# Additions first in VectorE's turn, in the three later edge stages of a four-layer graph network

## The chip, the cores and the metric

The kernel runs on one core of a Trainium2 chip. The metric is the device time in microseconds (us); of the kernel before there are three timed runs, and one more execution was profiled. A core has five engines that run side by side and wait for each other by semaphores: TensorE (PE in the profile, with PEld for its weight loads), VectorE (DVE), ScalarE (ACT), GpSimd (POOL) and SyncE (SP).

## The reference

Four layers, each a graph layer and a dense mixer side by side and then a feed-forward part. The edge sums of layers 1 to 3 are what the change touches (the mixer and feed-forward parts are left out here):

```
xn = _layernorm(x)
# layer 1, relation graph: a weighted mean by (relation, target)
msg = xn[src] * edge_weight[:, None]
h = segment_sum(msg, edge_type * N + dst) / count ;  out = einsum('rnc,rco->no', h, weight) + xn @ root + bias
# layer 2, isomorphism graph
agg = segment_sum(edge_weight[:, None] * xn[src], dst)
# layer 3, graph attention
h = xn @ W ;  e = exp(-leaky_relu((h @ a1)[src] + (h @ a2)[dst], 0.2))
h_prime = segment_sum(e[:, None] * h[dst], src) / segment_sum(e, src)[:, None]
```

There are 3125 nodes of 256 values and 50000 edges.

## The kernel before, in words

The nodes are cut into 25 tiles of 125 (`P`). The edges are sorted by the tile of the node that they are summed into, and padded, so that a run of 512 edges (`by_dst`, grain 512) or of 256 (`by_src`, grain 256) belongs to one tile. A group is 512 edges, 4 units of 128 (`GT` = 4). `edge_stage` (line 1346) goes over the groups three times in the program: as `g1e` (mode "relation", 124 groups), as `g2e` (mode "weight", 124 groups) and as `g3e` (mode "gat", 110 groups). With grain 512 a group has one sum (`sums` = 1), with grain 256 it has two (`sums` = 2).

For a group, these steps are made:

- POOL gathers the rows of the 4 units from DRAM by indirect DMA (line 1418), into one of six buffers (`GOTS` = 6). A buffer is free again when the sums of the group six before it are complete (`summed`).
- VectorE makes one-hot rows of the edges' target nodes (`place`, line 1562). TensorE turns them (`pt`, line 1460), ScalarE brings them to SBUF (`placet`, line 1444), and TensorE fetches with them each edge's value of its tile (`pq`, line 1488). From `pq` VectorE works out one coefficient for each edge (lines 1536 to 1540 in mode "gat", 1544 to 1553 in mode "relation", called the coefficients below), and ScalarE multiplies the one-hots by it (`placew`, line 1437; in mode "gat" after an exponential, line 1431). In mode "weight" none of this is needed: VectorE makes `placew` itself in 4 instructions (line 1527).
- TensorE multiplies: `pa` (PSUM, `adds` = 2 banks in turn) becomes the sum over the units of `placew`, turned, times the gathered rows (line 1474). This is the sum.
- VectorE adds the sum from PSUM to the node tile in SBUF (line 1575, the addition). The tile's number was loaded to a register before (line 1566).

The order is written out by hand, as a software pipeline over turns n. In turn n TensorE does `pt` of group n+3, `pa` of n, `pq` of n+2, and a step of a mixer. ScalarE does `placew` of n+1, `placet` of n+3, and a step of the mixer. VectorE does the coefficients of n+1 (or `placew` of n+2), `place` of n+4, the additions of n-1, and a step of the mixer. The mixer (`side`: `SoftmaxMixer`, `HeadNormMixer`, `SquaredMixer`) is a coroutine that is advanced one step by each engine in each turn; its tiles are named `m_...`.

The waits around the addition are these. VectorE's addition of sum x waits for `summed` x+1, and TensorE's `pa` of sum x waits for `added` x-1, since with two banks it writes over sum x-2. So with one sum to a group, `pa` of group n waits for the addition of group n-2; with two sums to a group (`g3e`), the first half of `pa` of group n waits for the first addition of group n-1. The coefficients of n+1 wait for `pq` of n+1, which stands behind `pa` of n-1 in TensorE's program, and `pq` of n+2 waits for the coefficients of n+1, as it has one PSUM buffer. `placew` of n+2 in mode "weight" waits for the sum of n-1.

Of the kernel before, what the change touches and what calls it, by code (L numbers as in the profile page):

```python
# [18 lines left out]
ALU = mybir.AluOpType  # L19
ACT = mybir.ActivationFunctionType  # L20
AX = mybir.AxisListType
ds = bass.ds
# [3 lines left out]
NT = N // P  # L26
# [592 lines left out]
def advance(program):  # L619

    if program is not None:
        next(program, None)


def run_out(program):

    if program is not None:
        for _ in program:
            pass
# [716 lines left out]
def edge_stage(nc, R, name, mode, b, acc, width, table, idx=R_IDX, spread=None, side=None, clear=True):  # L1346
# [10 lines left out]
    groups = b.units // GT  # L1357
    each = b.grain // 128
    sums = GT // each
    wide = table.shape[1]  # L1360
    PART = -(-groups // PARTS)
    turns, adds, ahead = 1, 2, 5
    with ExitStack() as ctx:
        def sem(n):
            return nc.alloc_semaphore(f"{name}_{n}")
# [22 lines left out]
        pa = [ctx.enter_context(nc.psum_tensor(f"{name}_pa{k}", [P, 512], F32)) for k in range(adds)]  # L1388
# [3 lines left out]
        split, placed, weighed, turned, evacuated, spreaded, logit, summed, added = (sem(n) for n in names)  # L1392
        block = ctx.enter_context(nc.Block())

        def fetched(g):

            return got_in[g % GOTS], 16 * GT * (g // GOTS + 1)

        @block.sync
        def _(sp):  # L1400
            view = b.rec[0:b.units * 128, :].rearrange("(p u) r -> p u r", p=128)
            for c in range(PARTS):
                at = slice(c * PART * GT, min(b.units, (c + 1) * PART * GT))
                sp.dma_start(rc[:, at, :], view[:, at, :]).then_inc(rec_in[c], 16)
            if side is not None:
                side.sync(sp)
            for c in range(PARTS):
                sp.wait_ge(rec_in[c], 16)
# [85 lines left out]
        @block.vector  # L1494
        def _(dve):
            tile_regs = [dve.alloc_register(f"{name}_dve_tile{k}") for k in range(sums)]
            own = side.vector(dve) if side is not None else None
            if clear:
                dve.memset(acc, 0.0)
            dve.tensor_copy(identb[:, :], R.identf[:, :])  # L1500
            if spreads:
                whole = spread.rearrange("p (t e) -> p t e", e=sw)
                dve.tensor_copy(rest[:, :, :], whole)
                dve.drain()
                for piece in range(3):
                    dve.tensor_copy(pieces[:, :, piece, :], rest[:, :, :])
                    dve.drain()
                    if piece < 2:
                        dve.tensor_tensor(rest[:, :, :], rest[:, :, :], pieces[:, :, piece, :], ALU.subtract)
                        dve.drain()  # L1510
                dve.sem_inc(split, 1)
            dve.drain()

            def ready(g):

                if g % PART == 0:
                    dve.wait_ge(rec_in[g // PART], 16)

            for n in range(1 - ahead, groups + 1):
                g = n + 2  # L1520
                if mode == "weight" and 0 <= g < groups:
                    ready(g)
                    if g >= 3:
                        dve.wait_ge(summed, (g - 2) * sums)
                    for j in range(GT):
                        u = g * GT + j
                        dve.tensor_scalar(placew[:, g % 3, j, :], R.iota[:, 0:P], rcf[:, u, b.loc:b.loc + 1],
                                          rcf[:, u, R_W:R_W + 1], ALU.is_equal, ALU.mult)
                    dve.drain().then_inc(weighed, 1)
                g = n + 1  # L1530
                at = slice(g * GT, (g + 1) * GT)
                if spreads and 0 <= g < groups:
                    dve.wait_ge(spreaded, g + 1)
                    if mode == "gat":
                        dve.wait_ge(*fetched(g))
                        dve.tensor_reduce(coef2[:, g % 4, :], pq[g % turns][:, 0:GT, 0:3], AX.X, ALU.add)
                        dve.drain()
                        dve.tensor_tensor(coef[:, g % 4, :], coef2[:, g % 4, :], got[:, g % GOTS, :, wide - 1], ALU.add)
                        dve.drain()
                        dve.scalar_tensor_tensor(out=coef[:, g % 4, :], in0=coef[:, g % 4, :], scalar=0.2,  # L1540
                                                 in1=coef[:, g % 4, :], op0=ALU.mult, op1=ALU.max)
                    else:
                        rels = [128, GT, 8]
                        dve.tensor_tensor(rel[:, g % 2, :, :], R.iota[:, 0:8].rearrange("p (a e) -> p a e", a=1).broadcast_to(rels),
                                          rcf[:, at, R_REL:R_REL + 1].broadcast_to(rels), ALU.is_equal)
                        dve.drain()
                        dve.tensor_tensor(small[:, g % 2, :, :, :], pq[g % turns][:, 0:GT, 0:24].rearrange("p j (n e) -> p j n e", e=8),
                                          rel[:, g % 2, :, :].rearrange("p j (a e) -> p j a e", a=1).broadcast_to([128, GT, 3, 8]),
                                          ALU.mult)
                        dve.drain()  # L1550
                        dve.tensor_reduce(coef2[:, g % 4, :], small[:, g % 2, :, :, :].rearrange("p j n e -> p j (n e)"), AX.X, ALU.add)
                        dve.drain()
                        dve.tensor_tensor(coef[:, g % 4, :], coef2[:, g % 4, :], rcf[:, at, R_W], ALU.mult)
                    dve.drain().then_inc(logit, 1)
                g = n + ahead - 1
                at = slice(g * GT, (g + 1) * GT)
                if spreads and g < groups:
                    ready(g)
                    if g >= ahead:
                        dve.wait_ge(weighed, g - ahead + 1)  # L1560
                    nodes = [128, GT, P]
                    dve.tensor_tensor(place[:, g % ahead, :, :], R.iota[:, 0:P].rearrange("p (a e) -> p a e", a=1).broadcast_to(nodes),
                                      rcf[:, at, b.loc:b.loc + 1].broadcast_to(nodes), ALU.is_equal)
                if n >= 1:
                    for x in range((n - 1) * sums, n * sums):
                        dve.reg_load(tile_regs[x % sums], b.tile_of[0:1, x:x + 1])
                if g < groups:
                    dve.drain().then_inc(placed, 1)
                g = n - 1
                if g >= 0:  # L1570
                    for x in range(g * sums, (g + 1) * sums):
                        to = dve.snap(tile_regs[x % sums], min_val=0, max_val=NT - 1)
                        dve.wait_ge(summed, x + 1)
                        into = acc[:, ds(to * width, width)]
                        dve.tensor_tensor(into, into, pa[x % adds][:, 0:width], ALU.add)
                        dve.drain().then_inc(added, 1)  # L1576
                if n >= -3:
                    advance(own)
            run_out(own)
# [1876 lines left out]
```

## Time and profile before

| | us |
|---|---|
| median of 3 runs (lowest to highest) | 7272.29 (7267.86 to 7276.22) |
| the profiled execution | 7262.79 |
| its span | 7261.1 |
| `g1e`: first gather to last addition | 3160.6 to 3900.6 |
| `g2e`: the same | 4423.8 to 5150.2 |
| `g3e`: the same | 6100.4 to 6831.7 |

The durations below come from the profiled execution, which lies 9.5 us (0.13%) under the median. The busy shares over the whole span (PE 58%, DVE 48%, ACT 26%, POOL 41%) are means over some thirty stages with different limits; for a change in one stage only the rows of that stage count. In rows of groups the figures are: line, engine, operation, out<-in, count | busy us, mean ns of one | idle us of the engine just before them, and what ended it. In a timeline a row is: start, length, engine, line, operation, out<-in, count, and in brackets the idle time before it with the releaser that was inferred for it. "issue" is idle time with nothing found that was waited for, "remote" a releaser that was not found.

### The profile page before, as it was taken

The page shows a single profiled execution, that of the slowest core. Times are in us where ns is not written, and L with a number is a line of the kernel's source. Part 1 is how long each engine was busy: PE and PEld are TensorE (multiplying, and loading weights), DVE is VectorE, ACT ScalarE, POOL GpSimd, SP SyncE. Part 2 cuts the span into 40 slices and gives each one's busy share as a digit, 9 for nine tenths or more (in the row PEclk, how much of TensorE's full clock was granted, in tenths as well). Part 3 has the DMA queues.
Part 4 walks back from the last instruction along what each step waited for, and adds up shares of the span by engine and source line. Part 5 has one row for each costly group of instructions (what it writes and reads, how often), then busy time and mean ns, then how long its engine had stood idle before and what let it go on. Part 6 is the DMA issues. An engine that isn't in the chain of part 4 may idle for free. (4 is left out here: it accounts for less than half of the span.)

```text
span 7261.1 us, 68529 instructions
## 1 busy us (share of the span) xinstructions
PE 4243.7 (58%) x17811; PEld 2977.3 (41%) x17811; DVE 3507.8 (48%) x8561; ACT 1885.5 (26%) x4934; POOL 2998.9 (41%) x3029
## 2 busy tenths in 40 slices
PE   0022567777775693766664843554439964676428
PEld 0000334444443572334443642343228852454315
DVE  6800578888887313436453034632361115554461
ACT  0000056666664120023342110000012211443201
POOL 0677033333331364046662734666104433665200
PEclk9985678888887796878876976776759986988759
DMA  1001033333332373233334322334315642332200
GB/s 38 3 17 27 9 90 100 96 100 97 98 99 55 118 212 103 102 122 89 91 91 61 100 58 89 92 92 92 39 38 174 189 134 75 90 88 79 33 21 18
DMA packets 361250, 602.13 MB, mean 83 GB/s; under 512 B 119031, under 2 KB 245096, under 8 KB 357376
## 3 DMA queue, kind: packets, MB, share of 16 engines
q0 software_dynamic: 162496, 359.47, 20.5%
q1 hardware_dynamic: 198386, 238.43, 10.1%
q8 instruction: 148, 2.42, 0.1%
q14 instruction: 220, 1.80, 0.1%
HBM read 518.82 MB, written 78.64 MB: 82 GB/s over the span
## 5 line engine op out<-in xcount | busy, mean ns | idle before, releaser
L1665 POOL DMA_INDIRECT g0e_got<-g_table,g0e_rc x496 | 474.2, 956 | 1071.0 <-DVEq L1825 730.2
L1418 POOL DMA_INDIRECT g1e_got<-g_table,g1e_rc x496 | 491.0, 990 | 525.0 <-DMA g1e_rc<-rec_dst 294.1
L1418 POOL DMA_INDIRECT g2e_got<-g_table,g2e_rc x496 | 478.5, 965 | 338.8 <-issue 140.7
L1418 POOL DMA_INDIRECT g3e_got<-g_table,g3e_rc x440 | 430.9, 979 | 357.7 <-issue 117.4
L1474 PE MATMUL g2e_pa<-g2e_got,g2e_placew 128*125 128x256 f32 x992 | 341.8, 507 | 376.1 <-DVEq L1576 186.5
L250 POOL DMA_INDIRECT rec_dst<-bydst_rc,bydst_sloti x391 | 402.8, 1030 | 296.0 <-DVEq L442 175.4
L2628 PE MATMUL f_p<-f_w2s,f_hid 128*128 128x256 f32 (+1 forms) x2176 | 498.8, 386 | 43.4 <-ACT f_hid L2648 35.0
L1753 PE MATMUL g0e_spread<-g0e_expanded,g0e_by_tile 128*125 128x512 bf16 x992 | 417.1, 510 | 177.3 <-ACT g0e_spaced L1702 141.6
L2617 PE MATMUL f_p<-f_xt,f_w1s 128*128 128x256 f32 (+1 forms) x2176 | 493.7, 384 | 20.0 <-DMA f_b2s<-in_L_ffn_b 8.0
L1702 ACT ACTIVATE g0e_spaced<-g0e_spread 125x512 bf16<-125x512 f32 x992 | 499.4, 627 | 20.6 <-remote 7.4
L2648 ACT ACTIVATE f_hid<-f_p,f_b1s 128x256 f32<-128x256 f32 (+1 forms) x544 | 251.7, 471 | 861.0 <-PE f_p L2617 493.6
L2628 PEld LDWEIGHTS f_p<-f_w2s,f_hid 128*128 128x128 f32 (+1 forms) x2176 | 408.2, 191 | 120.1 <-ACT f_hid L2648 64.1
L2617 PEld LDWEIGHTS f_p<-f_xt,f_w1s 128*128 128x128 f32 x2176 | 416.9, 193 | 86.2 <-DMA f_b2s<-in_L_ffn_b 17.0
L250 POOL DMA_INDIRECT rec_src<-bysrc_rc,bysrc_sloti x391 | 379.9, 972 | 119.2 <-issue 119.2
L1474 PEld LDWEIGHTS g2e_pa<-g2e_got,g2e_placew 128*125 128x125 f32 x992 | 239.1, 252 | 463.0 <-issue 414.2
L1474 PE MATMUL g3e_pa<-g3e_got,g3e_placew 128*125 128x257 f32 x880 | 279.0, 472 | 190.9 <-ACTq L1438 108.2
L508 PE MATMUL ln_pt<-identf,XN 125*128 125x125 f32 x200 | 43.6, 363 | 532.1 <-DVE XN L486 372.7
L2583 POOL DMA_INDIRECT f_got<-f_rows,f_of_slot x176 | 185.6, 1055 | 409.1 <-PE f_pt L2605 282.8
L1808 DVE TENSOR_TENSOR g0e_spaced<-g0e_spaced 125x2048 bf16<-125x2048 bf16 x496 | 326.8, 659 | 54.3 <-ACT g0e_spaced L1702 7.7
L1759 PE MATMUL g0e_pa<-g0e_msg,g0e_place 128*125 128x272 f32 x992 | 342.4, 504 | 3.0 <-DVEq L1843 3.0
L1474 PE MATMUL g1e_pa<-g1e_got,g1e_placew 128*125 128x256 f32 x992 | 310.9, 468 | 12.2 <-DMA g1e_got<-g_table,g1e_rc 6.5
L1753 PEld LDWEIGHTS g0e_spread<-g0e_expanded,g0e_by_tile 128*125 128x125 bf16 x992 | 139.7, 151 | 405.7 <-ACT g0e_spaced L1702 367.5
(656 smaller groups left out, 8265.3 us busy)
## 6 DMA issues: line engine op xcount, KB each, us to landing
f_w1s<-in_L_ffn_W SPq DMA_DIRECT2D x32, 1024.0 KB
f_w2s<-in_L_ffn_W SPq DMA_DIRECT2D x32, 1024.0 KB
g_table<-g1t_out SPq DMA_DIRECT2D x25, 1000.0 KB
f_w1s<-in_L_ffn_w SPq DMA_DIRECT2D x40, 512.0 KB
f_w2s<-in_L_ffn_w SPq DMA_DIRECT2D x40, 512.0 KB
f_results<-f_y SPq DMA_DIRECT2D x72, 256.0 KB
f_b2s<-in_L_ffn_b SPq DMA_DIRECT2D x80, 128.0 KB
f_rows<-XN SPq DMA_DIRECT2D x3, 3125.0 KB
```

Of the source, the lines that this page charges most:

```text
L250: pool.indirect_dma_start(self.rec, bass.IndirectOffsetOnAxis(self.sloti[:, c:c + 1], 0), self.rc[:, c, :], None).then_inc(scattered, 16)
L1418: pool.indirect_dma_start(got[:, g % GOTS, j, :], None, table, bass.IndirectOffsetOnAxis(rc[:, g * GT + j, idx:idx + 1], 0))\
L1474: last = pe.matmul(pa[x % adds][:, 0:width], placew[:, g % 3, j, :], got[:, g % GOTS, j, 0:width], start=(j % each == 0), stop=(j % each = ...
L1665: pool.indirect_dma_start(got[:, s, j, :], None, table, bass.IndirectOffsetOnAxis(rc[:, sl, j, R_IDX:R_IDX + 1], 0)).then_inc(got_in[s], 16)
L1702: act.activation(spaced[:, j, h:h + 4, :], spread[:, u % 3, :].rearrange("p (h e) -> p h e", e=128), ACT.Copy).then_inc(copied, 1)
L1753: pe.matmul(spread[:, u % 3, :], by_tile[:, j, :], expanded[:, s % 2, h:h + 4, :], start=True, stop=True).then_inc(spread_out, 1)
L1759: last = pe.matmul(pa[:, 0:W], place[:, s, j, :], msg[:, s % 2, j, :], start=(j == 0), stop=(j == GT - 1))
L1808: dve.tensor_tensor(a, a, b, ALU.max)
L2583: pool.indirect_dma_start(got[:, s % 2, j, :], None, rows, bass.IndirectOffsetOnAxis(of_slot[:, s * TJ + j:s * TJ + j + 1], 0))\
L2617: last = pe.matmul(p1[n % 4][:, 0:TS], w1s[:, weights_of(s), c, f * 128:(f + 1) * 128], xt[:, s % 2, c, :], start=(c == 0), stop=(c == KC ...
L2628: last = pe.matmul(p2[n % 2][:, 0:D], hid[:, f, j * RP:(j + 1) * RP], w2s[:, weights_of(s), f, :], start=(f == 0), stop=(f == NF - 1))
L2648: act.activation(hid[:, f, :], p1[n % 4][:, 0:TS], func, bias=b1s[:, weights_of(s), f:f + 1])\
```

## The change

In VectorE's turn of `edge_stage` the block of additions moves from behind the one-hots to the place behind `placew` of mode "weight" and ahead of the coefficients and of `place`. The register load of a sum's tile number stays behind `place`, but now loads the number of the group that is added at the head of the next turn. No instruction that computes is added or left out; TensorE, ScalarE, POOL and SyncE have the program that they had.

```diff
                     dve.drain().then_inc(weighed, 1)
+                g = n - 1
+                if g >= 0:
+                    for x in range(g * sums, (g + 1) * sums):
+                        to = dve.snap(tile_regs[x % sums], min_val=0, max_val=NT - 1)
+                        dve.wait_ge(summed, x + 1)
+                        into = acc[:, ds(to * width, width)]
+                        dve.tensor_tensor(into, into, pa[x % adds][:, 0:width], ALU.add)
+                        dve.drain().then_inc(added, 1)
                 g = n + 1
 ...
-                if n >= 1:
-                    for x in range((n - 1) * sums, n * sums):
+                if 0 <= n < groups:
+                    for x in range(n * sums, (n + 1) * sums):
                         dve.reg_load(tile_regs[x % sums], b.tile_of[0:1, x:x + 1])
                 if g < groups:
                     dve.drain().then_inc(placed, 1)
-                g = n - 1
-                if g >= 0:
-                    for x in range(g * sums, (g + 1) * sums):
-                        to = dve.snap(tile_regs[x % sums], min_val=0, max_val=NT - 1)
-                        dve.wait_ge(summed, x + 1)
-                        into = acc[:, ds(to * width, width)]
-                        dve.tensor_tensor(into, into, pa[x % adds][:, 0:width], ALU.add)
-                        dve.drain().then_inc(added, 1)
                 if n >= -3:
```

VectorE in `g3e`, late in the stage, one turn before the change (L905 is the mixer's last kind of step, X<-m_pa and X<-m_pt in turn; TENSOR_LOAD is the register load, ISA the register move):

```order
L905 SCALAR_TENSOR_TENSOR X<-m_pt,m_s,X 125x256
L1536 TENSOR_REDUCE g3e_coef<-g3e_pq 128x4
L1538 TENSOR_TENSOR g3e_coef<-g3e_coef,g3e_got 128x4
L1540 SCALAR_TENSOR_TENSOR g3e_coef<-g3e_coef 128x4
L1562 TENSOR_TENSOR g3e_place<-iota,g3e_rc 128x500
L1566 TENSOR_LOAD tile_src x2
L1575 ISA
L1575 TENSOR_TENSOR g_acc<-g_acc,g3e_pa 125x257
L1575 ISA
L1575 TENSOR_TENSOR g_acc<-g_acc,g3e_pa 125x257
L905 SCALAR_TENSOR_TENSOR X<-m_pa,m_s,X 125x256
```

The same turn of VectorE now (lines behind the new block are 8 further down, the additions are at line 1536):

```order
L905 SCALAR_TENSOR_TENSOR X<-m_pt,m_s,X 125x256
L1536 ISA
L1536 TENSOR_TENSOR g_acc<-g_acc,g3e_pa 125x257
L1536 ISA
L1536 TENSOR_TENSOR g_acc<-g_acc,g3e_pa 125x257
L1544 TENSOR_REDUCE g3e_coef<-g3e_pq 128x4
L1546 TENSOR_TENSOR g3e_coef<-g3e_coef,g3e_got 128x4
L1548 SCALAR_TENSOR_TENSOR g3e_coef<-g3e_coef 128x4
L1570 TENSOR_TENSOR g3e_place<-iota,g3e_rc 128x500
L1574 TENSOR_LOAD tile_src x2
L905 SCALAR_TENSOR_TENSOR X<-m_pa,m_s,X 125x256
```

The two additions went from the end of the turn, behind three coefficient instructions and the one-hots, to its head. `g1e` moves in the same way, with one addition and four coefficient instructions.

VectorE in `g2e`, a turn before the change:

```order
L1527 TENSOR_SCALAR g2e_placew<-iota,g2e_rc 128x125 x4
L1566 TENSOR_LOAD tile_dst
L1575 ISA
L1575 TENSOR_TENSOR g_acc<-g_acc,g2e_pa 125x256
L996 TENSOR_REDUCE m_mean<-XN 125x8
```

And now:

```order
L1527 TENSOR_SCALAR g2e_placew<-iota,g2e_rc 128x125 x4
L1536 ISA
L1536 TENSOR_TENSOR g_acc<-g_acc,g2e_pa 125x256
L1574 TENSOR_LOAD tile_dst
L996 TENSOR_REDUCE m_mean<-XN 125x8
```

Here only the register load changed places with the addition.

## Rows read from the trace of the kernel before

**Rows 1.** Groups of instructions by line, whole span.
```profile
L1418 POOL DMA_INDIRECT g1e_got<-g_table,g1e_rc x496 | 491.0, 990 | 525.0 <-DMA g1e_rc<-rec_dst 294.1 <-issue 136.5 <-remote 82.1
L1418 POOL DMA_INDIRECT g2e_got<-g_table,g2e_rc x496 | 478.5, 965 | 338.8 <-issue 140.7 <-DMA g2e_rc<-rec_dst 110.8 <-DMA rec_src<-bysrc_rc,bysrc_sloti 78.9
L1418 POOL DMA_INDIRECT g3e_got<-g_table,g3e_rc x440 | 430.9, 979 | 357.7 <-issue 117.4 <-PE g3e_pa L1474 99.8 <-DMA g3e_rc<-rec_src 93.4
L1474 PE MATMUL g3e_pa<-g3e_got,g3e_placew 128*125 128x257 f32 x880 | 279.0, 472 | 190.9 <-ACTq L1438 108.2 <-DVEq L1576 58.9 <-issue 22.8
```

**Rows 2.** Busy us (xinstructions) by stretch of `g3e`: PE, PEld, DVE, ACT, POOL; clock, DMA, GB/s.
```profile
6200.00:6600.00 400.00, 286.84 (x1372) 199.31 (x1370) 210.89 (x622) 169.13 (x509) 255.66 (x267) 0.92 0.32 89
6600.00:6830.00 230.00, 146.17 (x615) 112.16 (x616) 78.41 (x224) 67.49 (x194) 105.10 (x108) 0.78 0.31 63
```

**Rows 3.** Waits of POOL, 6650 to 6800: us in total, times, longest us.
```profile
POOL g3e_got L1418 <- PE g3e_pa L1474: 52.6, 20, 3.8
```

**Rows 4.** Timeline of `g3e`, one late turn and the start of the next.
```profile
6703.86 0.48 DVE L905 SCALAR_TENSOR_TENSOR X<-m_pa,m_s,X 125x256 f32<-125x256 f32 x1 [5.25 <-PE m_pa L758]
6704.53 0.17 DVE L1536 TENSOR_REDUCE g3e_coef<-g3e_pq 128x4 f32<-128x12 f32 x1 [0.19 <-issue]
6705.31 0.68 DVE L1562 TENSOR_TENSOR g3e_place<-iota,g3e_rc 128x500 bf16<-128x500 f32 x1
6705.52 1.27 ACT L1437 ACTIVATE g3e_placew<-g3e_place,g3e_expd 128x125 f32<-128x125 bf16 x4
6706.30 0.42 DVE L1575 TENSOR_TENSOR g_acc<-g_acc,g3e_pa 125x257 f32 x1 [0.31 <-issue]
6706.89 3.17 PE L1474 MATMUL g3e_pa<-g3e_got,g3e_placew 128*125 128x257 f32 x8 [2.66 <-ACTq L1438]
...
6707.02 0.42 DVE L1575 TENSOR_TENSOR g_acc<-g_acc,g3e_pa 125x257 f32 x1 [0.30 <-issue]
...
6710.01 1.55 PE L758 MATMUL m_pt<-m_M,XNT 128*125 128x256 f32 x4
...
6711.60 0.48 DVE L905 SCALAR_TENSOR_TENSOR X<-m_pt,m_s,X 125x256 f32<-125x256 f32 x1 [4.16 <-PE m_pt L758]
```

**Rows 5.** Timeline of `g3e`, from the middle of the stage.
```profile
6311.22 0.17 DVE L1536 TENSOR_REDUCE g3e_coef<-g3e_pq 128x4 f32<-128x12 f32 x1 [0.21 <-PE g3e_pq L1488]
...
6312.99 0.42 DVE L1575 TENSOR_TENSOR g_acc<-g_acc,g3e_pa 125x257 f32 x1 [0.31 <-issue]
6313.58 1.97 PE L1474 MATMUL g3e_pa<-g3e_got,g3e_placew 128*125 128x257 f32 x8 [1.33 <-ACTq L1438]
...
6315.50 1.96 PE L726 MATMUL m_pa<-m_w,XNT 128*125 128x512 f32 x4
...
6321.19 0.69 DVE L845 TENSOR_TENSOR m_vx<-m_pa,m_bias 125x512 f32<-125x512 f32 x1 [2.61 <-DMA g2e_got<-g_table,g2e_rc]
```

**Rows 6.** Timeline of `g2e`, one turn.
```profile
4578.58 1.11 DVE L1527 TENSOR_SCALAR g2e_placew<-iota,g2e_rc 128x125 f32<-128x125 f32 x4
4580.42 0.42 DVE L1575 TENSOR_TENSOR g_acc<-g_acc,g2e_pa 125x256 f32 x1 [0.73 <-issue]
4581.02 1.96 PE L1474 MATMUL g2e_pa<-g2e_got,g2e_placew 128*125 128x256 f32 x8 [0.47 <-issue]
```

**Rows 7.** Timeline of `g1e`, after a stall.
```profile
3341.21 0.19 DVE L1544 TENSOR_TENSOR g1e_rel<-iota,g1e_rc 128x32 f32<-128x32 f32 x1 [2.18 <-remote]
3342.66 0.26 PE L1488 MATMUL g1e_pq<-g1e_pieces,g1e_placet 125*128 x4 [1.55 <-DVEq L1554]
```

**Rows 8.** Waits in `g1e`, 3150 to 3900.
```profile
DVE g1e_rel L1544 <- remote: 169.8, 51, 18.2
PE g1e_pq L1488 <- issue: 44.1, 21, 5.1
PE g1e_pq L1488 <- DVEq L1554: 41.0, 28, 4.4
DVE g1e_rel L1544 <- PE g1e_pq L1488: 32.4, 18, 9.8
```

## The prediction

> **What bounds the kernel now.** I read the groups by line first, because the three changed stages each have one line of gathers there. A gather keeps POOL 0.98 us and a free POOL starts the next after 0.27 us: in `g3e` (430.9 + 117.4) / 440 = 1.25 us, so 4.98 us for a group of four [rows 1]. That is the floor of a turn. Measured is more. In the middle of `g3e` 267 gathers take 400 us, 5.99 us a group [rows 2]; late in the stage POOL waits once in each group, 20 times in 150 us, so 7.5 us a group [rows 3]. The idle time of POOL in `g3e` beyond its first wait and its issue time is 357.7 - 117.4 - 93.4 = 147 us, nearly all of it waits for sums. It is the most that the stage can give back. The same figure is 338.8 - 140.7 - 110.8 = 87 us in `g2e` and 525.0 - 294.1 - 136.5 = 94 us in `g1e` [rows 1].
>
> Next the timeline, to see what the sums wait for. Late in `g3e` the ring is plain [rows 4]: the mixer's matmul on TensorE, VectorE's X (3.86), its coefficients (4.53), the one-hots (5.31), the first addition (6.30 to 6.72), and 0.17 us behind it `pa` (6.89), then the next mixer matmul (10.01 to 11.56), X again (11.60): 7.74 us round. The profile puts `pa`'s wait down to ScalarE, whose `placew` ended at 6706.79. By the code that is the wrong one: this `placew` belongs to the group behind, and what `pa` needs from its own turn is the first addition of the group before. In the middle of the stage the same distance stands: addition 6312.99 + 0.42, `pa` at 6313.58, again 0.17 later [rows 5]. I went through the stage turn by turn, and `pa` follows the end of the first addition by 0.15 to 0.2 us wherever TensorE isn't busy. So the 190.9 us that TensorE waits before `pa` in `g3e` [rows 1] are mostly waits for an addition that stands behind the coefficients and one-hots of other groups.
>
> **The change, part by part.** No work is added. I sum against the profiled execution, 7262.8 us, and shift the result by the 9.5 us that it lies under the median.
>
> Late `g3e`. From X's start to `pa` are 6706.89 - 6703.86 = 3.03 us. Now X (0.48), a gap, the addition (0.42) and 0.17 us remain. The gap is 0.19 us (before the coefficients) to 0.31 us (before the addition) [rows 4]; I take 0.3, so 1.37 us, 1.66 saved. At 7.5 to 7.7 us a turn the 230 us from 6600 hold some 30 turns, of which the last three have no mixer step: 27 x 1.66 = 45 us. What is late next? `pa`'s second half waits for the second addition, 0.72 us after the first (6.30 to 7.02), and its first half lasts at least 0.98 us (half of 1.97, rows 5), so it is covered. `placew` comes later by both additions, 1.44 us: coefficients to the end of `placew` were 6706.79 - 6704.53 = 2.26 us, now 3.7 from the head of the turn, and are needed one `pa` later, in the next turn. The turn would be about 6.0 us, still above 4.98.
>
> Middle of `g3e`. The gain is bounded by the floor: 5.99 - 4.98 = 1.0 us a turn, 78 us over the 78 turns between the start and 6600. From below it is nothing: in most turns VectorE is busy all round (0.21 us idle ahead of the coefficients [rows 5]), and a turn of VectorE is as long as before, only turned round. What is left are the turns in which VectorE waits in a mixer step, about one in three: `m_vx` waits 2.61 us at 6321.19 [rows 5], for a matmul recorded from 6315.50 to 6317.46. TensorE would start that matmul up to 1.3 us sooner (its whole idle time before `pa`, rows 5). 26 such turns x 1.3 = 34 us, and I take that. That the wait ended 3.7 us after the recorded end of the matmul I can't explain; if something else sets it, this term goes to nothing.
>
> `g2e`. The addition stays behind `placew`; only the register load leaves the path. The gap before the addition is 0.73 us [rows 6] against 0.30 where no load is exposed [rows 4]: 0.43 us sooner, and `pa` starts 0.18 us after an addition here too (4580.84 to 4581.02). But the load then delays what follows the addition by as much, and VectorE's turn is as long. From nothing to 0.43 x 124 / 2 = 27 us (an addition lets the sum after next start, so half). I take 8, nearer to nothing, since a turn of VectorE with a mixer step has no room.
>
> `g1e`. Here TensorE hardly waits before `pa`, and the path runs over the coefficients: they wait 51 + 18 times, 202 us, and `pq` of the next group waits for them, 28 times with VectorE named and 21 times with nobody named [rows 8]. After a stall VectorE starts the coefficients at once (3341.21) and `pq` follows at 3342.66 [rows 7]. With the addition in front, its 0.42 and a gap of 0.30 come between, 0.72 us, unless the sum was ready during the wait. The sum stands ahead of `pq` in TensorE's program, so the addition never waits longer than the coefficients did; but in many stalls both seem to be released together. Cost: 28 x 0.72 = 20 us taken; 49 x 0.72 = 35 from above; a gain of 5 from below, where the addition fills the wait.
>
> The Trainium skill (TensorE: Matmul & The Clock Gate, "Architectural detail: the array is 16× 32×32, not 1× 128×128") says that VectorE's queue is a strict FIFO, so an addition that waits would hold the coefficients behind it: this is the rule that speaks against the change. By that alone `g1e` would pay in all 69 of its waits, 50 us, and the sum below would be 30 us poorer.
>
> Sum: -45 - 34 - 8 + 20 = -67 us. 7262.8 - 67 = 7195.8 on the profile's footing, 7272.3 - 67 = 7205 as a median.
>
> **Rivals.** First, only the late turns gain. For it: most middle turns have VectorE as their ring, and the `m_vx` wait ends at a time that no recorded end explains. Against: TensorE does idle 1.33 us before `pa` there. Then -45 - 0 - 0 + 20 = -25: 7247.
>
> Second, the whole of `g3e` falls to the gathers' pace: -147, with +20 and -8 for the others, so -135: 7137. For it: the granted clock is 0.78 late in the stage against 0.92 in the middle [rows 2], `pa` takes 3.17 us there [rows 4] against 1.97 [rows 5], and a TensorE that idles less could come to the higher level: another 1.2 us a turn, x 27 = 32 us; and with six buffers a turn faster than 4.98 us makes up for a slow one. Against: the middle stalls would have to go wholly. The Trainium skill (the same page, "The HAM clock gate") says that idleness halves TensorE's clock and activity gives it back; by that the late turns would gain more than my term.
>
> Third, slower: the coefficients are the ring in `g3e` too. Then `placew`, named by the profile for 108.2 us of the waits before `pa`, is what `pa` waits for, and both additions (1.44 us) go in front of it in each of the 27 late turns, +39, and `g1e` pays 35: +74, 7346. It decides where the turn's head to `placew`'s end, 3.7 us, exceeds what the turn leaves. The 0.17 us distance to the addition in the middle and late speaks against it.
>
> Fourth, it cancels: late turns win half (the mixer's matmul or `placet`, now 1.44 us later, becomes late), -23, and `g1e` pays 20: about 7269. That the change doesn't move what it says is ruled out by the order.
>
> **How the numbers follow.** The forecast 0.45 (own range 7180 to 7230), only late turns 0.20, gathers' pace 0.20, it cancels 0.08, slower 0.07. The range 7125 to 7264 takes in the forecast, the second and nearly all of the first, and reaches down to the middle term's full bound. About 0.2%, 14.5 us, is what a measurement of this kernel can tell from no change. Faster by more than that: 0.45 + 0.20 + 0.19 = 0.84; within it 0.09; slower 0.07.
>
> **What would show it.** In late `g3e`: addition 0.3 us behind X, `pa` 0.17 us behind the addition, the ring 6.0 us or less instead of 7.74, and POOL's waits for sums in 6650 to 6800 down from 52.6 us to about 20. The wait before `pa` in `g3e` falls from 190.9 us to under 90. In the middle: more than 267 gathers in 400 us, about 290. In `g2e`: a gap of about 0.3 us before the addition, the stage 0 to 27 us shorter. In `g1e`: the wait of `pq` for the coefficients grows, the stage is up to 35 us longer. The forecast is wrong if `pa` in `g3e` comes later than 0.3 us after the first addition, and ScalarE's `placew` ends just ahead of it; or if `g1e` grows by more than 40 us.

## The result, and the profile after

The changed kernel takes 7224.96 us (median of 4 runs, 7218.54 to 7231.76) where the kernel before takes 7274.26 us beside it. The ratio is 0.9933, with an interval of 0.9918 to 0.9949: 49 us faster, between 37 and 60. The profiled execution took 7222.27 us with a span of 7220.6 us; that is 40.5 us under the span of before.

First the groups by line of the changed kernel, over the whole span (busy us, mean ns | idle us before them, and what ended it).

```profile
L1418 POOL DMA_INDIRECT g1e_got<-g_table,g1e_rc x496 | 478.4, 965 | 539.0 <-DMA g1e_rc<-rec_dst 294.5 <-issue 133.0 <-remote 73.9
L1418 POOL DMA_INDIRECT g2e_got<-g_table,g2e_rc x496 | 478.3, 964 | 339.0 <-issue 140.0 <-DMA g2e_rc<-rec_dst 111.0 <-DMA rec_src<-bysrc_rc,bysrc_sloti 83.3
L1418 POOL DMA_INDIRECT g3e_got<-g_table,g3e_rc x440 | 428.4, 974 | 327.0 <-issue 118.9 <-DMA g3e_rc<-rec_src 92.7 <-remote 67.6
L1474 PE MATMUL g3e_pa<-g3e_got,g3e_placew 128*125 128x257 f32 x880 | 261.3, 447 | 63.6 <-DVEq L1537 36.0 <-issue 26.4 <-ACTq L1438 1.1
```

Against [rows 1]: only `g3e`'s idle time of POOL fell, from 357.7 to 327.0 us, and the wait before `pa` fell from 190.9 to 63.6 us, four times as much. Taken from the first gather's start to the last addition's start, `g1e` went from 739.6 to 741.3 us, `g2e` from 726.0 to 727.4, `g3e` from 730.8 to 685.9. The sum of the three, -41.9 us, is the whole change of the span (-40.5). In `g3e` 32.5 us of it lie between the first and the last gather, and 12.4 us behind the last gather, where the groups still in the buffers run out (36.5 us before, 24.1 after).

The stretches of `g3e`, to be held against [rows 2] (us, then busy us (xinstructions) of PE, PEld, DVE, ACT, POOL; clock; DMA; GB/s). The second ends where the additions end:

```profile
6200.00:6600.00 400.00, 298.44 (x1378) 207.52 (x1377) 212.48 (x625) 171.06 (x512) 256.72 (x267) 0.87 0.32 89
6600.00:6790.00 190.00, 126.21 (x625) 93.83 (x624) 81.02 (x232) 70.28 (x201) 107.26 (x111) 0.88 0.46 79
```

The middle holds 267 gathers in 400 us, exactly as before: it gained nothing. POOL's waits of over 0.7 us there add up to 74 us before and 75 us now. The late part does 111 gathers in 190 us where before needed 230 for 108. The late turns on the timeline, against [rows 4]:

```profile
6700.97 0.48 DVE L905 SCALAR_TENSOR_TENSOR X<-m_pt,m_s,X 125x256 f32<-125x256 f32 x1 [0.87 <-PE m_pt L758]
...
6701.75 0.42 DVE L1536 TENSOR_TENSOR g_acc<-g_acc,g3e_pa 125x257 f32 x1 [0.30 <-issue]
...
6702.64 1.98 PE L1474 MATMUL g3e_pa<-g3e_got,g3e_placew 128*125 128x257 f32 x8 [0.43 <-DVEq L1537]
...
6704.56 1.11 PE L758 MATMUL m_pa<-m_M,XNT 128*125 128x256 f32 x4
...
6706.16 0.48 DVE L905 SCALAR_TENSOR_TENSOR X<-m_pa,m_s,X 125x256 f32<-125x256 f32 x1 [1.63 <-PE m_pa L758]
...
6706.95 0.42 DVE L1536 TENSOR_TENSOR g_acc<-g_acc,g3e_pa 125x257 f32 x1 [0.30 <-issue]
...
6707.55 1.97 PE L1474 MATMUL g3e_pa<-g3e_got,g3e_placew 128*125 128x257 f32 x8 [0.90 <-issue]
...
6712.11 0.48 DVE L905 SCALAR_TENSOR_TENSOR X<-m_pt,m_s,X 125x256 f32<-125x256 f32 x1 [2.37 <-DMA f_back<-f_results,f_slot]
```

The addition starts 0.30 us behind X. These two turns are 5.19 us (6700.97 to 6706.16) and 5.95 us, where the one in [rows 4] was 7.74, but turns differ, so here are all 24 between the first and the last X of the stage:

| mean of 24 turns, us | before | changed |
|---|---|---|
| X's start to `pa`'s start | 3.10 | 1.48 |
| `pa`'s own time | 3.04 | 2.39 |
| `pa`'s end to the next X | 1.32 | 1.94 |
| turn (shortest to longest) | 7.45 (5.96 to 9.33) | 5.81 (4.44 to 7.25) |

In most of them `pa` follows the first addition by 0.18 us and X by 1.38 us, as in the second turn shown; in the first it comes 0.47 us behind the addition, where `pt`, which stands before it in TensorE's program, ran until 6702.21.

In the middle the gain went elsewhere. TensorE's groups in 6200 to 6600, first of the kernel before:

```profile
L1474 PE MATMUL g3e_pa<-g3e_got,g3e_placew 128*125 128x257 f32 x531 | 150.8, 433 | 79.3 <-ACTq L1438 40.8 <-DVEq L1576 28.0 <-issue 9.5
...
L708 PE MATMUL m_pc<-m_k,m_vx 125*128 125x256 f32 x89 | 30.1, 468 | 17.6 <-ACTq L777 17.5
```

and of the changed one:

```profile
L1474 PE MATMUL g3e_pa<-g3e_got,g3e_placew 128*125 128x257 f32 x530 | 153.2, 438 | 6.6 <-DVEq L1537 6.6
...
L708 PE MATMUL m_pc<-m_k,m_vx 125*128 125x256 f32 x88 | 38.1, 578 | 74.7 <-ACTq L777 68.2 <-issue 6.5
```

The wait before `pa` went from 79.3 to 6.6 us, and the wait before the mixer's `m_pc` from 17.6 to 74.7. `m_pc` needs the keys `m_k`, which ScalarE norms behind `placew` and `placet` of the same turn; these wait for coefficients that now stand behind two additions.

What else holds the middle is seen on the timeline of the changed kernel, in a stop of the kind that ends more than half of POOL's 43 waits over 0.7 us in 6200 to 6600:

```profile
6346.13 0.39 PE L1460 MATMUL g3e_pt<-g3e_identb,g3e_place 128*125 128x128 bf16 x4
...
6346.36 1.95 PE L1474 MATMUL g3e_pa<-g3e_got,g3e_placew 128*125 128x257 f32 x8
...
6349.65 0.99 POOL L1418 DMA_INDIRECT g3e_got<-g_table,g3e_rc  x1 [0.30 <-issue]
...
6352.10 0.60 ACT L1444 ACTIVATE g3e_placet<-g3e_pt 125x512 bf16<-125x512 bf16 x1 [2.90 <-remote]
6352.27 0.42 DVE L1536 TENSOR_TENSOR g_acc<-g_acc,g3e_pa 125x257 f32 x1 [2.44 <-remote]
6352.45 0.94 POOL L1418 DMA_INDIRECT g3e_got<-g_table,g3e_rc  x1 [1.81 <-remote]
...
6353.26 2.05 PE L708 MATMUL m_pc<-m_k,m_vx 125*128 125x256 f32 x4 [4.87 <-ACTq L777]
```

ScalarE waits for `pt`, recorded as done at 6346.52, and VectorE and POOL for `pa`, recorded as done at 6348.31. All three go on within 0.35 us, at 6352.10 to 6352.45, 4 to 5.6 us after the recorded ends. (Ends of matmuls in the profile are modelled.) I call this a stop. The profile names such waits "remote". They are in both kernels.

In `g2e` the addition starts 0.30 us behind `placew` in 118 of 124 turns, where it was 0.73, but the time comes back in front of the mixer's first instruction:

```profile
4581.35 1.11 DVE L1527 TENSOR_SCALAR g2e_placew<-iota,g2e_rc 128x125 f32<-128x125 f32 x4
4582.76 0.42 DVE L1536 TENSOR_TENSOR g_acc<-g_acc,g2e_pa 125x256 f32 x1 [0.30 <-issue]
4583.73 0.17 DVE L1010 TENSOR_SCALAR m_var<-m_var 125x8 f32<-125x8 f32 x1 [0.55 <-issue]
...
4586.48 1.11 DVE L1527 TENSOR_SCALAR g2e_placew<-iota,g2e_rc 128x125 f32<-128x125 f32 x4
```

This turn of VectorE is 5.13 us long (4581.35 to 4586.48), and the same turn before is 5.13 too (4578.58 to 4583.71). In `g1e` the moved waits balance as well. VectorE's waits in `g1e` of the changed kernel (3160 to 3905; us in total, times, longest us):

```profile
DVE X L1536 <- remote: 110.0, 38, 18.3
DVE X L1536 <- PE g1e_pa L1474: 77.8, 31, 5.3
DVE X L1536 <- issue: 27.7, 42, 9.2
DVE g1e_rel L1552 <- remote: 26.7, 10, 5.7
```

The 202 us of waits before the coefficients [rows 8] are now 188 us before the addition and 27 us (remote) before the coefficients. TensorE's wait before `pq` grew, from 85.1 to 117.6 us, and its wait before `pt` fell, from 157.6 to 115.5 us.

### The profile page after: what moved, and what is told of

Read it like the earlier page. It is cut to its first block and busy times, and to the rows that moved or that the text cites. A ratio compares the mean times of both kernels' runs of the same rounds, so it can differ in the third digit from the quotient of the medians.

```text
span 7220.6 us, 68529 instructions
## 1 busy us (share of the span) xinstructions
PE 4234.4 (59%) x17811; PEld 2964.4 (41%) x17811; DVE 3508.7 (49%) x8561; ACT 1884.0 (26%) x4934; POOL 2983.0 (41%) x3029
## 5 line engine op out<-in xcount | busy, mean ns | idle before, releaser
L1418 POOL DMA_INDIRECT g3e_got<-g_table,g3e_rc x440 | 428.4, 974 | 327.0 <-issue 118.9
L1474 PE MATMUL g3e_pa<-g3e_got,g3e_placew 128*125 128x257 f32 x880 | 261.3, 447 | 63.6 <-DVEq L1537 36.0
```

What stands on the lines that cost most here:

```text
L1418: pool.indirect_dma_start(got[:, g % GOTS, j, :], None, table, bass.IndirectOffsetOnAxis(rc[:, g * GT + j, idx:idx + 1], 0))\
L1474: last = pe.matmul(pa[x % adds][:, 0:width], placew[:, g % 3, j, :], got[:, g % GOTS, j, 0:width], start=(j % each == 0), stop=(j % each = ...
```

## Experiments

In the first four the kernel before takes 7313 us beside them, in the next four 6797 us and in the last four 6798. I write "the first chip" for where it takes over 7200 us and "the second chip" for where it takes 6800, but what differs there isn't known: the record gives the first four and the next four runs the same chip number, 14 (of the same machine or not), and the last four number 2. So totals are compared as ratios to the kernel before, taken beside them, and stages only within the first or the second. "Stage" is first gather's start to last addition's start.

**Additions first in `g3e` only.** `- if g >= 0:` `+ if mode == "gat" and g >= 0:` at the head of the turn, the old place for the other two stages.

> Additions open VectorE's turn only in g3e; g1e and g2e keep the order of before. Theory (the whole gain is the late part of g3e, and g1e and g2e pay nothing): g3e 686 us, the ratio to before 0.993 (7225), equal to the full change within 3 us. Rival (g1e pays the 20 us of the prediction, hidden by luck elsewhere): this kernel is 15 to 20 us faster than the full change, near 7205.

Ratio 0.9923 (0.9906 to 0.9939). `g3e` 695.7 us, `g1e` 749.9, `g2e` 734.9. The whole gain is `g3e`'s; the kernel is not measurably apart from the full change (0.9933). The rival's 7205 would have been 0.9905.

**Additions first in `g1e` only.** The same with `mode == "relation"`.

> Additions open the turn only in g1e. Theory: the addition is done in a wait that was there anyway, g1e 740 to 743 us as before, total within 0.1% of before (7267 to 7280). Rival (the price of 0.72 us in 28 stalls): g1e 760, total 7294.

Ratio 0.9997 (0.9986 to 1.0007): no change. `g1e` 750.9 us against 749.9 with the old order on the same chip; `g3e`, here in the old order, 751.9 against 695.7 in the first experiment. The two experiments below give `g1e` 751.1 us in the new order and 751.2 in the old, so 1 us is within the scatter of single profiles: `g1e` pays nothing that can be seen, not 20 us. On this chip `g3e` gains 56 us.

**The mixer's keys one turn sooner, on the changed kernel and on the kernel before.**

```diff
             turned(t)
-            yield
             keys(t)
             yield
+            yield
```

> The changed kernel, and in the mixer that runs beside g3e ScalarE norms a tile's keys one turn sooner (m_k, in the turn of the transpose's evacuation). Theory (the middle of g3e gained nothing because TensorE's wait went from pa to m_pc, 74.7 us in 6200 to 6600, for keys that ScalarE norms behind placew of the same turn): the wait before m_pc falls under 15 us, the middle holds 290 or more gathers in 400 us instead of 267, g3e falls by 40 to 70 us, total 7155 to 7185. Rival (the middle is held by a late signal of the mixer's matmuls, or by VectorE's own turn of 5.9 us): the wait goes to another instruction, 267 gathers again, total 7225.

> The same edit of the mixer in the kernel before. Theory (before the change TensorE waits before pa for the addition, and only 17.6 us before m_pc): the middle gains at most a part of these 17.6 us, g3e 725 to 731, total 7266 to 7274. Rival (keys are the ring in both orders): g3e falls by as much as in the changed kernel, 40 us or more.

Changed kernel 0.9924 (0.9907 to 0.9940), kernel before 1.0000 (0.9991 to 1.0010). TensorE's groups of the changed kernel with this edit, 6230 to 6630:

```profile
L1474 PE MATMUL g3e_pa<-g3e_got,g3e_placew 128*125 128x257 f32 x531 | 156.7, 445 | 22.2 <-DVEq L1537 20.4 <-issue 1.6
L1460 PE MATMUL g3e_pt<-g3e_identb,g3e_place 128*125 128x128 bf16 x268 | 28.4, 231 | 67.1 <-ACT g3e_placet L1444 56.7 <-issue 10.1
L708 PE MATMUL m_pc<-m_k,m_vx 125*128 125x256 f32 x92 | 26.2, 408 | 0.0
```

The wait before `m_pc` is gone (the first experiment has 75.5 us there in the same stretch), and 67.1 us stand before `pt`. The stretch holds 267 gathers (265 in the first experiment), not 290. `g3e` is 688.8 us against 695.7: 7 us, not 40 to 70. (In the old order it is 748.1 with the edit and 751.9 without.) My theory that the keys hold the middle fell. On this chip a wait taken from one place comes out at the next, and what stays are the stops: of POOL's waits for sums in `g3e`, "remote" ones were 72.8 of 123.7 us without the edit and are 90.8 of 116.2 with it.

**Eight and four buffers for gathered groups.** `- GOTS = 6` `+ GOTS = 8`, or `4`, on the changed kernel.

> The changed kernel with eight buffers for gathered groups instead of six, in all three stages. What is asked: TensorE's signals (summed and the mixer's) sometimes come 2 to 5 us after the recorded end of its matmuls, and then POOL, VectorE and ScalarE all go on within 0.3 us. Theory A: such a stop ends only when POOL has run out of buffers and its last gather has landed (in the changed kernel 2.3 to 2.6 us after that gather's start, 3.5 us in g2e). Then more buffers only put the stops farther apart: still a stop of 2 to 3 us each, release at the same distance from the last gather, g2e one stop in about 30 us instead of 23, the three stages 20 to 35 us shorter each at most. Theory B: the stop has a length of its own, and the buffers either cover it or not: then nearly all of POOL's waits vanish, g3e falls to about 600 us, g2e to 640, total below 7100. Theory C: POOL's waits follow TensorE's mean pace, not its stops: nothing changes, 7225 on the footing of the first result.

> The changed kernel with four buffers for gathered groups instead of six. Theory A (a stop of TensorE's signals lasts until POOL's last gather has landed): stops come about twice as often in g2e (every 12 to 15 us) and each is as long as before, POOL's release again 2.3 to 3.5 us behind the start of its last gather; the stages grow by 30 to 90 us each. Theory B (a stop has a length of its own, 4 to 6 us): POOL waits longer in each, the release moves farther from the last gather, by up to 5 us. Theory C: no change.

0.9933 (0.9916 to 0.9949) and 0.9929 (0.9913 to 0.9946): both as the full change. What the runs show is another thing, in the groups by line with eight buffers:

```profile
L1418 POOL DMA_INDIRECT g1e_got<-g_table,g1e_rc x496 | 482.6, 973 | 444.1 <-DMA g1e_rc<-rec_dst 293.3 <-issue 147.7 <-PE g1e_pa L1474 3.0
L1418 POOL DMA_INDIRECT g2e_got<-g_table,g2e_rc x496 | 477.3, 962 | 261.7 <-issue 146.8 <-DMA g2e_rc<-rec_dst 110.9 <-PE g2e_pa L1474 4.0
L1418 POOL DMA_INDIRECT g3e_got<-g_table,g3e_rc x440 | 453.8, 1031 | 226.2 <-issue 131.9 <-DMA g3e_rc<-rec_src 92.5 <-PE g3e_pa L1474 1.8
```

On this chip POOL has no "remote" waits. It hardly waits for a sum, even with four buffers (9.3, 12.8 and 5.9 us in the three stages), and the stages take 660.5, 656.2 and 606.9 us. The question I asked, what ends a stop, could not be answered where there are none.

**X one turn later late in `g3e`,** on the changed kernel; ahead of the last loop of the mixer's part on VectorE: `+ yield`.

> The changed kernel, and in the late part of g3e VectorE adds a mixer tile to X one turn later, so that it no longer waits for a matmul of the same turn. Theory (late g3e is the ring X, addition, pa, pq, the mixer's matmul, X): VectorE's wait before X goes, the turn falls from 5.9 us to 5.0 to 5.3, g3e 15 to 25 us shorter than with the change alone. Rival (the late part is held by late signals like the middle): the wait before X moves to the addition, g3e within 5 us of the change alone.

0.9935 (0.9918 to 0.9952), stage 611.3 us, against 606.9 and 612.0 in two runs with eight buffers and 606.9 with four (the plain change, with six, has no profile on this chip): no gain, though the wait before X went. On this chip the changed `g3e` is already at the gathers' pace.

**The mixer beside `g3e` left out,** on the changed kernel (`X` keeps its old value there): `- side=SquaredMixer(...)`.

> The changed kernel with the mixer beside g3e left out (X keeps its old value). Theory (the middle is held by waits and late signals that come with the mixer's matmuls): g3e runs at the gathers' pace, 1.25 us each, about 620 us, and TensorE's signals come within 0.5 us of its recorded ends. Rival (they come with the gathers and have nothing to do with the mixer): stops stay, every 10 to 25 us, and g3e stays above 650 us.

One run, 6744.3 us, stage 609.5: as with the mixer. With the change the mixer costs `g3e` nothing on this chip. Whether the stops come with the mixer is open, for the same reason as above.

**Between coefficients and one-hots.** In `g3e` the additions stand ahead of `place` but behind the coefficients.

> As the changed kernel, but in g3e the additions stand between the coefficients and the one-hots. Theory (a late turn of g3e is X, what stands ahead of the first addition, addition, pa, mixer matmul): the coefficients (0.78 us from their start to the one-hots' start) come back into the ring, the late turns lose about half of the gain: about 20 of the 45 us, ratio to before 0.995 to 0.997. Rival (the gain comes only from the one-hots going behind the addition, or the coefficients must be early): as fast as the full change, 0.993.

0.9945 (0.9928 to 0.9961), stage 626.0 us; before 652.6, full change 607 to 612 (with four or eight buffers). Two late turns on the timeline of this kernel:

```profile
6232.02 0.48 DVE L905 SCALAR_TENSOR_TENSOR X<-m_pa,m_s,X 125x256 f32<-125x256 f32 x1 [3.37 <-PE m_pa L758]
6232.69 0.17 DVE L1544 TENSOR_REDUCE g3e_coef<-g3e_pq 128x4 f32<-128x12 f32 x1 [0.19 <-issue]
...
6233.65 0.42 DVE L1569 TENSOR_TENSOR g_acc<-g_acc,g3e_pa 125x257 f32 x1 [0.30 <-issue]
...
6234.24 3.01 PE L1474 MATMUL g3e_pa<-g3e_got,g3e_placew 128*125 128x257 f32 x8 [2.03 <-DVEq L1570]
...
6238.95 0.48 DVE L905 SCALAR_TENSOR_TENSOR X<-m_pt,m_s,X 125x256 f32<-125x256 f32 x1 [3.36 <-PE m_pt L758]
```

From X to `pa` are 2.22 us, against 3.03 before and 1.38 with the full change: the ring is as long as what stands ahead of the first addition. The turn is 6.93 us; over all 24 turns the mean is 6.83 us, against 7.50 before and 5.45 to 5.60 with the full change. The stage keeps 27 of the 41 to 46 us.

**X one turn later, on the kernel before.**

> The kernel before, and late in g3e VectorE adds a mixer tile to X one turn later. Theory (the ring of a late turn closes over X's wait for the mixer's matmul of the same turn): the ring is cut without the change, late turns fall from 7.7 us to 5 to 6, g3e is 30 to 50 us shorter, as much as the change brings. Rival (pa's wait for an addition behind coefficients and one-hots is enough by itself): 0 to 10 us.

0.9916 (0.9899 to 0.9932): 57 us faster, the lowest ratio of all, though its interval overlaps those of the full change. The kernel before, on the same chip, late in `g3e`:

```profile
6263.48 0.48 DVE L905 SCALAR_TENSOR_TENSOR X<-m_pa,m_s,X 125x256 f32<-125x256 f32 x1 [2.52 <-PE m_pa L758]
...
6271.06 0.48 DVE L905 SCALAR_TENSOR_TENSOR X<-m_pt,m_s,X 125x256 f32<-125x256 f32 x1 [4.00 <-PE m_pt L758]
```

and with X one turn later:

```profile
6222.65 0.48 DVE L906 SCALAR_TENSOR_TENSOR X<-m_pa,m_s,X 125x256 f32<-125x256 f32 x1
...
6225.85 0.42 DVE L1576 TENSOR_TENSOR g_acc<-g_acc,g3e_pa 125x257 f32 x1 [0.32 <-issue]
6226.45 1.97 PE L1475 MATMUL g3e_pa<-g3e_got,g3e_placew 128*125 128x257 f32 x8 [1.22 <-ACTq L1439]
...
6227.12 0.48 DVE L906 SCALAR_TENSOR_TENSOR X<-m_pt,m_s,X 125x256 f32<-125x256 f32 x1
```

X no longer waits, and the turn is 4.47 us instead of 7.58. Seventeen turns go by in 4.45 to 4.95 us; the last seven take 6.4 to 7.0, as the coefficients there wait for gathered rows to land. The stage is 592.6 us instead of 652.6. So the ring needed both its parts: the addition behind coefficients and one-hots, which the change moves, and X's wait for a matmul of its own turn, which this edit removes. Undoing either one is enough here; X one turn later on the old order was not run where there are stops.

**Eight buffers again, and the kernel before for its trace.**

> The changed kernel with eight buffers once more. The first run of it fell on a chip on which before takes 6797 us and POOL waits for sums nowhere, so the question stayed open. If before takes over 7200 us here: theory A (a stop of TensorE's signals ends when POOL has run out of buffers and its last gather has landed): the release stays 2.3 to 3.6 us behind the last gather's start and the stops come farther apart, g2e one in about 30 us, each stage 15 to 35 us shorter than with six buffers. Theory B (a stop has a length of its own): POOL's waits go almost wholly, each stage 60 us or more shorter. If before takes about 6800 us: 6751 again, nothing learned.

> The kernel before, for its trace on this chip. Theory (the late ring of 7.7 us is in the program, the late signals are in the chip): on a chip on which before takes about 6800 us, g3e holds its late turns of 7 to 7.7 us with 45 us of waits for sums, and the middle runs at 5.0 us a turn; on one over 7200 us the trace is that of the first profile, with 267 gathers in 400 us in the middle.

The first gave 0.9929 (0.9912 to 0.9945) and again no stop to look at. The second, the kernel before on this chip:

```profile
L1418 POOL DMA_INDIRECT g3e_got<-g_table,g3e_rc x440 | 438.6, 997 | 269.7 <-issue 121.1 <-DMA g3e_rc<-rec_src 92.7 <-PE g3e_pa L1474 55.9
```

and its stretch 5800 to 6200:

```profile
5800.00:6200.00 400.00, 303.45 (x1512) 213.73 (x1510) 230.18 (x677) 188.29 (x558) 300.89 (x307) 0.93 0.37 102
```

In the middle it does 307 gathers in 400 us (5.2 us a group), and POOL's waits for sums are mostly late: 42.3 of the 55.9 us lie in 6200 to 6340, in 17 waits. The same program does 267 in the first profile. The late ring is in the program, with a mean turn of 7.50 us here and 7.45 in the first profile; the six microseconds a turn of the middle are not, as they are here only 5.2. With the change the same stretch holds 299 to 302 gathers (eight and four buffers), so there was nothing to win in the middle here either.

## Why the prediction was right or wrong

The forecast, 7205, stands 20 us below the 7225 measured; the range and the sign hold. The time lies halfway to the first rival (only late turns gain, 7247). By terms:

**Late `g3e`, -45.** Right in mechanism: `g3e` is 44.9 us shorter, with the addition 0.30 us behind X, a mean turn of 5.81 us where 6.0 was forecast, and POOL's waits for sums in 6650 to 6800 down from 52.6 us [rows 3] to 16.9 + 4.7. The orders in between show the ring term by term (X to `pa` 3.03, 2.22, 1.38). That the size is right to a tenth of a microsecond is partly luck. I counted 27 turns at 1.66 us; there are 24 between the first and the last X, at 1.64, which is 39.4 us, and the other 5.5 lie ahead of them (2.5) and behind them (3.0). And two things that the term leaves out cancelled: `pa` itself became 0.65 us shorter, and the way from its end to the next X 0.62 us longer.

The first of these goes with the clock. Late in the stage the granted clock rose from 0.78 to 0.88. In the kernel before on the second chip the turn from 6257.4 to 6263.5 has a granted clock of 1.00 (the upper of the two levels, 2.4 GHz, throughout), a `pa` of 1.97 us and takes 6.1 us; the next has 0.77 (partly at the lower, 1.2 GHz), a `pa` of 3.46 us and takes 7.58. The Trainium skill (TensorE: Matmul & The Clock Gate, "The HAM clock gate") says that idleness costs clock and activity gives it back. Late, the trace agrees. In the middle it doesn't: TensorE was busy for 298 us of 400 instead of 287, and the granted clock fell, from 0.92 to 0.87; why is open.

**Middle `g3e`, -34.** Wrong: nothing. The step that failed is "TensorE would start that matmul up to 1.3 us sooner". It did idle less before `pa`, but most of that time came back two instructions on, before `m_pc` (79.3 + 17.6 = 96.9 us before, 6.6 + 74.7 = 81.3 after). The remark that "the wait ended 3.7 us after the recorded end of the matmul" was the sign to follow: the runs on the second chip show that without such stops the middle is near the gathers' pace in either order. I had given that case its price, nothing. What makes the stops stays open.

**`g2e`, -8.** Wrong: nothing. The gap ahead of the addition fell to 0.30 us as forecast; the stage grew by 1.4 us, within scatter (734.3 us in the new order, 734.4 to 735.5 in the old, in the first four experiments). The step that failed is that an earlier addition lets the sum after next start earlier; the remark that the load then delays what follows by as much is what the trace shows, with 0.55 us in front of the mixer's first instruction. On the second chip `g2e` is near the gathers' pace, so there was nothing to win there.

**`g1e`, +20.** Mis-sized: +1.7, and +1.0 in the experiment that isolates it, both within scatter. I took 28 stalls at 0.72 us for exposed. Sum and `pq` are mostly signalled together: behind the addition only 15 of 124 turns still wait before the coefficients, where 69 waited. `pq` did come later, its wait grew by 32.5 us (by 38.4 in the experiment), but the wait before the next `pt` fell by 42.1 us (36.0), so the stage didn't pay. Which of the stage's waits sets its length was not tried. The addition stands in front of the coefficients and takes over their wait, 188 us of it. The Trainium skill (the same page, "Architectural detail: the array is 16× 32×32, not 1× 128×128") states that VectorE's queue is a strict FIFO. The trace agrees with the order, but not with the 50 us that I priced by it.

**The slower rival** (coefficients and `placew` are the ring in `g3e`) fell: `placew` is named for 1.1 us of `pa`'s waits now, after 108.2.

The errors, 43 us too much gain (34 in the middle, 9 in `g2e`) and 18 us too much cost, partly cancelled: that the forecast lies only 20 us off is luck. The terms as measured are -45 + 0 + 1 + 2 = -42, or 7230.

## What to carry to other kernels

Look for the ring, not for the longest wait. A ring closes over several engines, and an order on one engine or a delay of a turn on another can cut it; before moving work in the main loop, see whether a side program waits for a result of its own turn, since one turn of slack there was one line and brought as much (57 us beside 45 to 52 for the change on the second chip; the intervals overlap). And before pricing a wait, ask what the waiting engine waits for next: of the 127 us that left `pa`, 45 reached the end.

## What the runs showed of the hardware

- The same program takes 7274 and 7313 us, or 6797 (what differs isn't known). In the first two TensorE's signals come in stops, up to 5.6 us after the recorded ends of its matmuls, with VectorE, ScalarE and POOL released together. In the third there is none: in `g2e` POOL's idle time is 262 us against 339, and the 79 us that the profile puts down to a DMA of `rec_src` [rows 1] are gone. The three edge stages together are 228 us shorter there, and the first gather of `g1e` starts 198 us sooner. What holds the signals is open. In `g3e` of the changed kernel 26 of 35 late releases of POOL come 2.4 to 2.9 us behind the start of its last gather; in the traces that record it (the second chip's) a gather's data lands 2.8 us after its start. Whether the one ends the other is not shown: there was no stop in the runs with more and with fewer buffers.
- A gather takes 0.95 us, but often 1.1 to 1.4 where it meets VectorE's one-hots. With the additions first and eight buffers, 101 of 440 gathers took over 1.05 us, 68 of them among the 115 that overlap a one-hot instruction; in the old order 54 of 440. That is 453.8 against 438.6 us of POOL, which is the limit there. It accounts for X one turn later doing better on the old order (stage 592.6) than on the new (611.3): POOL is idle for 226.3 us in both and busy for 435.8 against 456.2, though the totals are not apart by their intervals. Overlap alone is not the cause, as in the changed kernel's first profile only 20 of 140 overlapping gathers took over 1.05 us.
